# Row maxima over 8 tiles of 112 queries in place of 7 tiles of 128, in a fused cross-attention and expert kernel on one core

## The chip, the core and the metric

The kernel runs on one core of a Trainium2 chip. Times are device microseconds (us). The engines are TensorE (PE, its weight loads PEld), VectorE (DVE), ScalarE (ACT), GpSimd (POOL) and SyncE (SP), which issues most of the DMAs.

## The reference, cut to what matters

```python
q = layernorm(x) @ Wq.T + bq                  # x: 16 batches x 224 queries x 512
k, v = ctx @ Wk.T + bk, ctx @ Wv.T + bv       # ctx: 16 x 750 keys x 384
attn = softmax(einsum('bihd,bjhd->bhij', q, k) * SCALE)   # 16 heads of 32
x = x + (einsum('bhij,bjhd->bihd', attn, v) @ Wo.T + bo)
x = x + top2_of_8_experts(layernorm(x))       # routing, gelu, two matmuls per expert
```

The softmax subtracts the maximum of each row (one query of one head, over 750 keys) before the exponential.

## The kernel before, in words

Attention takes about three quarters of the time; routing and the experts follow and are not touched. Attention is cut into 64 groups: 16 batches by 4 groups of 4 heads. Each engine has its program written out by hand: four functions named `first`, `second`, `third` and `fourth` say what an engine does for a group with index 0, 1, 2 or 3 within its batch, and a loop over g from -2 to 68 calls them in turn. Semaphores are the only tie between engines, and each engine works strictly in the order of its program.

In iteration g the PE works on three groups at once:

- group g: `score(g, s)`, twelve steps of two matmuls each into one of two banks S (125 keys by 224 queries, for one head), which ACT turns into probabilities `pr` (`exps`, L781). Step s waits until ACT has read step s-2. `values(g, p)` multiplies the probabilities by v into O (16 small matmuls, L1558); `denominators(g - 1)` (L1569) waits for sums of the probabilities that POOL adds up (`add_step`, L475 and L478).
- group g+1: `score_for_max(g + 1, u)` (L1519) computes approximate scores with queries on the partitions, only to get the maxima. The 4 heads by 224 queries are 896 rows, cut into 7 tiles u of 128. A tile takes two matmuls of 376 keys each (a pair) into X, which is a single buffer of two banks: DVE's `maximum` (L1061) reduces both to one column of `mx`, and the next pair waits for that (`max_done`). After the last tile `transpose_max` (L1528) turns `mx` into rows in a bank of M; ACT negates them into `mneg` (L771), and a DMA from SP (`put_max`, L390) puts them as one row of 896 numbers under the stacked queries `qst`, so that the score matmuls of the next iteration subtract the maximum by themselves. `score(g + 1, 0)` waits for this DMA.
- group g+2: the projections of q and k, and once a batch v and the output (`project_q`, `project_k`, `project_v`, `project_o`, with their three matmuls a product at L314 to L316).

The order of `score_for_max` among the rest is written out. In all four functions tile 0 comes at or near the start and tile 6 about four fifths through; `transpose_max` stands next to the last scores. What stands between tile 6 and the transpose differs: `values(g, 1)` and scores everywhere, and besides the logits of the router in `first` (L1462), half of the output projection in `second`, transposes of y in `fourth` (L1447). Below, the part from tile 6 to the transpose is called the tail of a function, and the whole of what `score_for_max` adds for one u is a pair.

`q_own` (written by ACT, `own_done`) holds, for each of the 4 heads of a group, the group's queries with the other heads' rows set to zero. It is laid out as head, then query, so that a tile of 128 rows runs over the border between heads in some places.

Of the kernel before, what the change touches and what calls it, by code (L numbers as in the profile page):

```python
# [64 lines left out]
GROUPS = B * NG  # L65
SB, MB = 2, 3
OS = 5
XU = GH * NQ // P
LAST = 5
LN_STEPS, Y_STEPS = 8, 16  # L70
E, DE = 8, 256
# [48 lines left out]
def expert_phase(nc, x1_d, w1, b1, w2, b2, centroids, w_route, ident_d, gates_dram, out):  # L120
    x, ctxT, wqT, bq, wkT, bk, wvT, bv, woT, bo, ident, x1 = SCRATCH["attention"]
    with ExitStack() as es:
# [45 lines left out]
        y_T = sb("y_T", [P, DC, NQ])  # L168
        o_s = sb("o_s", [P, NQ])
        rw = sb("rw", [P, DC, 2 * E])  # L170
        mneg = sb("mneg", [XU, P], F32R)
        zone_end = here[0]

        bq_s, bk_s, bv_s = sb("bq_s", [P, NG]), sb("bk_s", [P, NG]), sb("bv_s", [P, NG])
# [159 lines left out]
        with nc.Block() as block:  # L334
# [350 lines left out]
            def _(act):  # L685
# [79 lines left out]
                def max_out(g):  # L765
                    if not 0 <= g < GROUPS:
                        return
                    wait_full(act, "mT", g)
                    if g:
                        act.wait_ge(m_in, 16 * g)  # L770
                    act.activation(mneg[:, :], bank_of("mT", g)[0:XU, 0:P], ACT.Copy, scale=-1.0).then_inc(freed("mT", g), 1)  # L771

                def exps(g, s):
                    if not 0 <= g < GROUPS:
# [235 lines left out]
            def _(dve):  # L1010
# [44 lines left out]
                def maximum(g, u):  # L1055
                    if not 0 <= g < GROUPS:
                        return
                    if u == 0 and g:
                        wait_full(dve, "mT", g - 1)
                    dve.wait_ge(x_full, XU * g + u + 1)  # L1060
                    dve.tensor_reduce(mx[:, u:u + 1], X[:, :, 0:HALF[0][1]], AX.XY, ALU.max).then_inc(max_done, 1)  # L1061

                def invert(g):
                    if not 0 <= g < GROUPS:
# [92 lines left out]
                def first(g, b):  # L1157
                    maximum(g + 1, 0)
                    q_lo(g + 2)
                    maximum(g + 1, 1)  # L1160
                    maximum(g + 1, 2)
                    k_lo(g + 2, 0)
                    maximum(g + 1, 3)
                    k_lo(g + 2, 1)
                    invert(g - 1)
                    normalise(g - 1)
                    maximum(g + 1, 4)
                    o_lo(g - 1)
                    maximum(g + 1, 5)
                    maximum(g + 1, 6)  # L1170
                    keep_logits(b - 2, 0)
                    keep_logits(b - 2, 1)

                def second(g, b):
                    maximum(g + 1, 0)
                    q_lo(g + 2)
                    maximum(g + 1, 1)
                    maximum(g + 1, 2)
                    k_lo(g + 2, 0)
                    maximum(g + 1, 3)  # L1180
                    k_lo(g + 2, 1)
                    xT_rest(b + 1, 0)
                    xT_rest(b + 1, 1)
                    invert(g - 1)
                    normalise(g - 1)
                    maximum(g + 1, 4)
                    o_lo(g - 1)
                    maximum(g + 1, 5)
                    residual(b - 1, 0)
                    maximum(g + 1, 6)  # L1190
                    residual(b - 1, 1)

                def third(g, b):
                    maximum(g + 1, 0)
                    q_lo(g + 2)
                    maximum(g + 1, 1)
                    maximum(g + 1, 2)
                    k_lo(g + 2, 0)
                    maximum(g + 1, 3)
                    k_lo(g + 2, 1)  # L1200
                    invert(g - 1)
                    normalise(g - 1)
                    maximum(g + 1, 4)
                    o_lo(g - 1)
                    maximum(g + 1, 5)
                    maximum(g + 1, 6)
                    y_stats(b - 1)

                def fourth(g, b):
                    maximum(g + 1, 0)  # L1210
                    q_lo(g + 2)
                    maximum(g + 1, 1)
                    maximum(g + 1, 2)
                    k_lo(g + 2, 0)
                    maximum(g + 1, 3)
                    k_lo(g + 2, 1)
                    invert(g - 1)
                    normalise(g - 1)
                    maximum(g + 1, 4)
                    o_lo(g - 1)  # L1220
                    maximum(g + 1, 5)
                    maximum(g + 1, 6)
                    ln_stats(b + 2)

                for g in range(-2, GROUPS + LAST):
# [193 lines left out]
            def _(pe):  # L1419
# [89 lines left out]
                def score_for_max(g, u):  # L1509
                    if not 0 <= g < GROUPS:  # L1510
                        return
                    own_q = q_own[:, g % 2, :, :].rearrange("p j n -> p (j n)")
                    if u == 0:
                        pe.wait_ge(kh_done, 2 * (g + 1))
                    pe.wait_ge(own_done, GH * g + (P * (u + 1) - 1) // NQ + 1)
                    if g or u:
                        pe.wait_ge(max_done, XU * g + u)
                    for i, (off, w) in enumerate(HALF):
                        last = pe.matmul(X[:, i, 0:w], own_q[:, P * u:P * (u + 1)],  # L1519
                                         kh_s[:, g % 2, off:off + w], start=True, stop=True)  # L1520
                    last.then_inc(x_full, 1)

                def transpose_max(g):
                    if not 0 <= g < GROUPS:
                        return
                    out, full = claim("mT", g)
                    pe.wait_ge(max_done, XU * (g + 1))
                    pe.transpose(out[0:XU, 0:P], mx[:, :], id_s[:, :]).then_inc(full, 1)  # L1528

                def score(g, s):  # L1530
                    if not 0 <= g < GROUPS:
# [75 lines left out]

                def first(g, b):
                    score_for_max(g + 1, 0)
                    project_q(g + 2)  # L1610
                    project_k(g + 2, 0)
                    score_for_max(g + 1, 1)
                    values(g - 1, 2)
                    score(g, 0)
                    score(g, 1)
                    score_for_max(g + 1, 2)
                    project_k(g + 2, 1)
                    score_for_max(g + 1, 3)
                    score(g, 2)
                    denominators(g - 1)  # L1620
                    project_v(b, 4, 0)
                    score_for_max(g + 1, 4)
                    score(g, 3)
                    score(g, 4)
                    project_v(b, 4, 1)
                    project_v(b, 5, 0)
                    score(g, 5)
                    project_v(b, 5, 1)
                    score_for_max(g + 1, 5)
                    score(g, 6)  # L1630
                    score(g, 7)
                    values(g, 0)
                    score(g, 8)
                    score_for_max(g + 1, 6)
                    values(g, 1)
                    score(g, 9)
                    logits(b - 2, 0)
                    logits(b - 2, 1)
                    score(g, 10)
                    score(g, 11)  # L1640
                    transpose_max(g + 1)

                def second(g, b):
# [26 lines left out]
                    score_for_max(g + 1, 6)  # L1670
                    project_o(b - 1, 1, 0)
                    score(g, 9)
                    project_o(b - 1, 1, 1)
                    score(g, 10)
                    score(g, 11)
# [2 lines left out]
                def third(g, b):  # L1678
                    project_q(g + 2)
                    score_for_max(g + 1, 0)  # L1680
                    project_k(g + 2, 0)
                    score_for_max(g + 1, 1)
                    score(g, 0)
                    values(g - 1, 2)
                    score(g, 1)
                    score_for_max(g + 1, 2)
                    project_k(g + 2, 1)
                    score(g, 2)
                    score_for_max(g + 1, 3)
                    project_v(b + 1, 0, 0)  # L1690
                    project_v(b + 1, 0, 1)
                    score(g, 3)
                    denominators(g - 1)
                    score_for_max(g + 1, 4)
                    project_v(b + 1, 1, 0)
                    score(g, 4)
                    score(g, 5)
                    project_v(b + 1, 1, 1)
                    score_for_max(g + 1, 5)
                    values(g, 0)  # L1700
                    score(g, 6)
                    score_for_max(g + 1, 6)
                    score(g, 7)
                    score(g, 8)
                    score(g, 9)
                    values(g, 1)
                    score(g, 10)
                    transpose_max(g + 1)
                    score(g, 11)

                def fourth(g, b):
# [27 lines left out]
                    score(g, 9)  # L1739
                    transpose_y(b - 1, 0)  # L1740
                    transpose_y(b - 1, 1)
                    score(g, 10)
                    transpose_max(g + 1)
                    score(g, 11)
# [125 lines left out]
```

## Time and profile before

| | |
|---|---|
| median of 3 runs | 1679.36 us (1679.16 to 1681.23) |
| the profiled execution | 1679.16 us, of which the span from first to last instruction is 1677.3 us |
| granted TensorE clock, mean over the span | 0.962 of full speed |
| PE busy | 1532.5 us, 91% |
| POOL / DVE / ACT busy | 65% / 58% / 56% |
| first and last pair of the row maxima | from 34.0 us to 1280.4 us |

The trace's times count from the span's start. A busy PE is not a PE at its peak, since matmuls overlap: the distance from one matmul's start to the next one's is what it costs in a row of them.

### The profile page before, as it was taken

To read this page: it belongs to the slowest core of one execution; us is meant where nothing else is said; L and a number is where in the kernel's file an instruction comes from. 1 tells how busy PE (TensorE), PEld (TensorE's weight loads), DVE (VectorE), ACT (ScalarE), POOL (GpSimd) and SP (SyncE) were. 2 spreads that over 40 slices of the span, in tenths; PEclk is the share of its full clock that TensorE was granted. 3 is DMA by queue.
4 is the path that set the end of the run, shared out by engine and by line. 5 is a ranking of instruction groups with operands and counts; after the bars stand their busy time and mean duration, and the time that the engine had idled before them with its cause. 6 is when DMAs were issued, how large, how long until landed. Compare 5 with 4: busy or idle time off the path is not lost.

```text
span 1677.3 us, 32844 instructions
## 1 busy us (share of the span) xinstructions
PE 1532.5 (91%) x11581; PEld 1256.8 (75%) x11581; DVE 973.8 (58%) x1464; ACT 935.6 (56%) x2048; POOL 1091.4 (65%) x947
## 2 busy tenths in 40 slices
PE   4899999999999999999999999999996439998997
PEld 4778787877877777778787877877774328887886
DVE  6555666566565656655666566565654574444665
ACT  4556665665666566666666666666554403553332
POOL 3377767767767777676767767777765514766553
PEclk9999999999999999999999999999997658998999
DMA  7564767676667676665767676657666416887663
GB/s 194 98 111 76 135 101 130 101 133 106 122 103 132 102 130 102 118 122 95 136 101 130 102 131 109 122 100 133 91 102 153 164 25 145 148 143 149 217 202 119
DMA packets 111372, 206.90 MB, mean 123 GB/s; under 512 B 19391, under 2 KB 48671, under 8 KB 111088
## 3 DMA queue, kind: packets, MB, share of 16 engines
q1 hardware_dynamic: 95456, 160.18, 52.2%
q0 software_dynamic: 15760, 44.63, 11.5%
q8 instruction: 100, 1.64, 0.4%
q14 instruction: 56, 0.46, 0.1%
HBM read 75.60 MB, written 35.00 MB: 66 GB/s over the span
## 4 chain that ended last, share of the span: by engine, by line
PE 63%; POOL 17%; issue 8%; ACT 4%; DVE 3%; DMA 3%; SPq 2%; POOLq 0%; DVEq 0%; ACTq 0%
POOL psum_p L478 11%; PE M L314 8%; PE S L1542 8%; PE M L315 8%; PE M L316 8%; PE X L1519 7%; PE O L1558 7%; POOL ctx_l L462 3%; ACT pr L781 2%; PE M L1569 2%; PE X L1782 2%; PE X L1781 2%; PE X L1783 2%; PE M L1802 1%; PE M L1800 1%
## 5 line engine op out<-in xcount | busy, mean ns | idle before, releaser
L478 POOL TENSOR_TENSOR psum_p<-psum_p,pr 125x896 f32<-125x896 f32 x256 | 542.3, 2118 | 174.1 <-ACT pr L781 150.8
L1061 DVE TENSOR_REDUCE mx<-X 128x1 f32<-128x752 f32 x448 | 421.4, 941 | 365.4 <-PE X L1519 363.3
L781 ACT ACTIVATE pr<-S 125x448 f32<-125x448 f32 x768 | 394.7, 544 | 215.7 <-PE S L1542 202.5
L1542 PEld LDWEIGHTS S<-qst,kst 128*125 128x125 f32 x1536 | 235.0, 189 | 123.7 <-ACT pr L781 60.0
L1542 PE MATMUL S<-qst,kst 128*125 128x224 f32 x1536 | 286.8, 291 | 39.1 <-ACT pr L781 26.5
L1519 PE MATMUL X<-kh_s,q_own 128*128 128x376 f32 x896 | 242.9, 352 | 5.5 <-DVE mx L1061 5.4
L1558 PE MATMUL O<-pr,v 125*32 125x224 f32 x3072 | 187.0, 362 | 1.9 <-ACT pr L781 1.9
L475 POOL TENSOR_TENSOR psum_p<-pr 125x896 f32<-125x896 f32 x64 | 135.1, 2112 | 82.1 <-ACT pr L781 81.9
L1519 PEld LDWEIGHTS X<-kh_s,q_own 128*128 128x128 f32 x896 | 146.5, 191 | 43.9 <-issue 34.8
L462 POOL TENSOR_TENSOR ctx_l<-ctx_r,ctx_h 128x750 fp32r<-128x750 f32 x48 | 85.3, 1807 | 75.8 <-ACT ctx_h L696 75.8
L314 PE MATMUL M<-ctx_h,wk_h 128*128 128x376 f32 (+1 forms) x384 | 128.9, 336 | 0.2 <-POOL ctx_l L462 0.2
L315 PE MATMUL M<-ctx_l,wk_h 128*128 128x376 f32 (+1 forms) x384 | 128.7, 335 | 0.0
L316 PE MATMUL M<-ctx_h,wk_l 128*128 128x376 f32 (+1 forms) x384 | 128.0, 333 | 0.0
L1068 DVE RECIPROCAL M<-M 128x224 f32<-128x224 f32 x64 | 99.8, 1560 | 47.8 <-PE M L1569 47.8
L1558 PEld LDWEIGHTS O<-pr,v 125*32 125x32 f32 x3072 | 80.8, 110 | 58.6 <-issue 21.2
L314 PE MATMUL M<-wv_h,ctx_h 128*125 128x512 f32 x288 | 116.9, 406 | 0.0
L315 PE MATMUL M<-wv_l,ctx_h 128*125 128x512 f32 x288 | 113.8, 395 | 0.0
L316 PE MATMUL M<-wv_h,ctx_l 128*125 128x512 f32 x288 | 113.6, 394 | 0.0
L738 ACT ACTIVATE q_own<-qh_s,own 128x224 fp32r<-128x224 f32 x256 | 102.6, 471 | 2.1
L1388 DVE TENSOR_TENSOR y_raw<-M,b_all 128x512 f32<-128x512 f32 x70 | 48.4, 692 | 83.6 <-PE M L1802 83.6
L632 POOL DMA_INDIRECT xg<-rows_d,table_x x40 | 41.9, 1048 | 76.4 <-ACT y_out L991 42.3
L1051 DVE SCALAR_TENSOR_TENSOR kl_s<-M,bk_s,kh_s 128x376 fp32r<-128x376 f32 (+1 forms) x128 | 77.2, 603 | 15.0 <-ACT kh_s L749 14.0
(217 smaller groups left out, 3161.5 us busy)
## 6 DMA issues: line engine op xcount, KB each, us to landing
kst<-kh_s SPq DMA_DIRECT2D x128, 375.0 KB, 7.4
kst<-kl_s SPq DMA_DIRECT2D x64, 375.0 KB, 10.4
ctx_r<-ctxT SPq DMA_DIRECT2D x48, 375.0 KB, 12.3
qst<-qh_s SPq DMA_DIRECT2D x128, 112.0 KB, 2.8
rows_d<-x_res SPq DMA_DIRECT2D x32, 448.0 KB, 11.4
w_l<-w SPq DMA_DIRECT2D x16, 512.0 KB, 10.0
x_ln<-x SPq DMA_DIRECT2D x16, 448.0 KB, 11.1
x_res<-x SPq DMA_DIRECT2D x16, 448.0 KB, 3.6
```

Source lines behind the costliest of these rows:

```text
L314: pe.matmul(out, lhs[0], rhs[0], start=first, stop=False)
L315: pe.matmul(out, lhs[0], rhs[1], start=False, stop=False)
L316: return pe.matmul(out, lhs[1], rhs[0], start=False, stop=last)
L462: pool.tensor_tensor(out=ctx_l[:, c, :], in0=ctx_r[:, c, :], in1=ctx_h[:, c, :], op=ALU.subtract).then_inc(ctx_lo, 1)
L475: pool.tensor_tensor(out=total, in0=tiles[0], in1=tiles[1], op=ALU.add).then_inc(sum_step, 1)
L478: pool.tensor_tensor(out=total, in0=total, in1=tiles[half], op=ALU.add).then_inc(sum_step, 1)
L738: act.activation(q_own[:, g % 2, j, :], qh_s[:, g % 2, :], ACT.Copy, scale=own[:, j:j + 1]).then_inc(own_done, 1)
L781: act.activation(pr[0:KP, (3 * g + p) % 2, j, :, :], S[0:KP, n % SB, 0:2 * NQ].rearrange("p (i n) -> p i n", i=2), ACT.Exp).then_inc(exp_d ...
L1061: dve.tensor_reduce(mx[:, u:u + 1], X[:, :, 0:HALF[0][1]], AX.XY, ALU.max).then_inc(max_done, 1)
L1519: last = pe.matmul(X[:, i, 0:w], own_q[:, P * u:P * (u + 1)], kh_s[:, g % 2, off:off + w], start=True, stop=True)
L1542: last = pe.matmul(S[0:KP, n % SB, NQ * h:NQ * (h + 1)], kst[:, i, j, o:o + KP], qst[:, i, j, :], start=True, stop=True)
L1558: last = pe.matmul(O[HD * j:HD * (j + 1), 0:NQ], v[0:KP, 2 * p + i, HD * j:HD * (j + 1)], pr[0:KP, (3 * g + p) % 2, j, i, :], start=(p == ...
```

## The change

The 896 rows are cut into 8 tiles of 112: tile u is head u // 2, half u % 2. The number of tiles `XU` goes from 7 to 8, matmuls, reduce, transpose and `mneg` work on 112 columns or partitions where they had 128, and each function of PE and DVE gets one more call, for u = 7. A tile lies within one head, so `own_done` is waited for only where a head begins.

```diff
-XU = GH * NQ // P
+XU = 8
-        mneg = sb("mneg", [XU, P], F32R)
+        mneg = sb("mneg", [XU, QP], F32R)
...
-                    dve.tensor_reduce(mx[:, u:u + 1], X[:, :, 0:HALF[0][1]], AX.XY, ALU.max).then_inc(max_done, 1)
+                    dve.tensor_reduce(mx[0:QP, u:u + 1], X[0:QP, :, 0:HALF[0][1]], AX.XY, ALU.max).then_inc(max_done, 1)
...
-                    own_q = q_own[:, g % 2, :, :].rearrange("p j n -> p (j n)")
+                    j, qt = u // QT, u % QT
                     if u == 0:
                         pe.wait_ge(kh_done, 2 * (g + 1))
-                    pe.wait_ge(own_done, GH * g + (P * (u + 1) - 1) // NQ + 1)
+                    if qt == 0:
+                        pe.wait_ge(own_done, GH * g + j + 1)
                     if g or u:
                         pe.wait_ge(max_done, XU * g + u)
                     for i, (off, w) in enumerate(HALF):
-                        last = pe.matmul(X[:, i, 0:w], own_q[:, P * u:P * (u + 1)],
+                        last = pe.matmul(X[0:QP, i, 0:w], q_own[:, g % 2, j, QP * qt:QP * (qt + 1)],
                                          kh_s[:, g % 2, off:off + w], start=True, stop=True)
...
-                    pe.transpose(out[0:XU, 0:P], mx[:, :], id_s[:, :]).then_inc(full, 1)
+                    pe.transpose(out[0:XU, 0:QP], mx[0:QP, :], id_s[0:QP, 0:QP]).then_inc(full, 1)
...
# DVE, at the end of each of the four functions, ahead of keep_logits, residual 1, y_stats, ln_stats:
                     maximum(g + 1, 6)
+                    maximum(g + 1, 7)
...
# PE, first, second (after score 9), third (after score 9), fourth (after transpose_y):
                     score(g, 9)
+                    score_for_max(g + 1, 7)
```

The PE's instructions at the end of `third`, from score 9 to the transpose, before:

```order
L1542 MATMUL S<-qst,kst 125x224 [waits exp_done]
L1542 MATMUL S<-qst,kst 125x224
L1558 MATMUL O<-pr,v_70 32x224 [waits exp_done]
L1558 MATMUL O<-pr,v_70 32x224 x7
L1542 MATMUL S<-qst,kst 125x224 [waits exp_done]
L1542 MATMUL S<-qst,kst 125x224
L1528 MATMUL M<-id_s,mx 7x128 [waits max_done,misc_free2]
```

and now:

```order
L1547 MATMUL S<-qst,kst 125x224 [waits exp_done]
L1547 MATMUL S<-qst,kst 125x224
L1524 MATMUL X<-kh_s,q_own 112x376 [waits max_done]
L1524 MATMUL X<-kh_s,q_own 112x376
L1563 MATMUL O<-pr,v_70 32x224 [waits exp_done]
L1563 MATMUL O<-pr,v_70 32x224 x7
L1547 MATMUL S<-qst,kst 125x224 [waits exp_done]
L1547 MATMUL S<-qst,kst 125x224
L1533 MATMUL M<-id_s,mx 8x112 [waits max_done,misc_free2]
```

A pair has come in ahead of `values(g, 1)`; between it and the transpose stand those matmuls and one score. At the end of `fourth` the PE has, before:

```order
L1447 MATMUL M<-id_s,x_res 128x112 [waits yn_done,misc_free1]
L1447 MATMUL M<-id_s,x_res 128x112 x3
L1542 MATMUL S<-qst,kst 125x224 [waits exp_done]
L1542 MATMUL S<-qst,kst 125x224
L1528 MATMUL M<-id_s,mx 7x128 [waits max_done,misc_free2]
```

and now, with the new pair between the transposes of y and score 10:

```order
L1451 MATMUL M<-id_s,x_res 128x112 [waits yn_done,misc_free1]
L1451 MATMUL M<-id_s,x_res 128x112 x3
L1524 MATMUL X<-kh_s,q_own 112x376 [waits max_done]
L1524 MATMUL X<-kh_s,q_own 112x376
L1547 MATMUL S<-qst,kst 125x224 [waits exp_done]
L1547 MATMUL S<-qst,kst 125x224
L1533 MATMUL M<-id_s,mx 8x112 [waits max_done,misc_free2]
```

## Rows read from the trace of the kernel before

**Rows 1.** The page: the chain that ended last, share of the span by engine.
```profile
PE 63%; POOL 17%; issue 8%; ACT 4%; DVE 3%; DMA 3%; SPq 2%; POOLq 0%; DVEq 0%; ACTq 0%
```
**Rows 2.** The page's groups: line, operation, count, busy and mean, idle before by releaser.
```profile
L1061 DVE TENSOR_REDUCE mx<-X 128x1 f32<-128x752 f32 x448 | 421.4, 941 | 365.4 <-PE X L1519 363.3
...
L1519 PE MATMUL X<-kh_s,q_own 128*128 128x376 f32 x896 | 242.9, 352 | 5.5 <-DVE mx L1061 5.4
```
**Rows 3.** Waits within attention (33 to 1285 us): total, times, longest.
```profile
PEld S L1542 <- issue: 40.9, 111, 1.1
PEld X L1519 <- issue: 34.8, 82, 1.6
...
PE S L1542 <- ACT pr L781: 23.9, 39, 2.3
```
**Rows 4.** The chain in order of time, `fourth`: start, us, what (x2 is one pair).
```profile
815.63 0.55 PE X L1519 x2
...
817.72 0.35 PE X L1519 x2
```
**Rows 5.** Timeline, end of `first`, PE and DVE: start, us, instruction, count [idle before].
```profile
849.04 0.94 DVE L1061 TENSOR_REDUCE mx<-X 128x1 f32<-128x752 f32 x1 [1.14 <-PE X L1519]
...
849.83 0.48 PE L1542 MATMUL S<-qst,kst 128*125 128x224 f32 x2
850.14 1.65 PE L1462 MATMUL M<-rw,y_T 128*112 128x16 f32 x16
...
852.15 0.27 PE L1528 MATMUL M<-id_s,mx 128*7 128x128 f32 x1
```
**Rows 6.** Timeline, PE, end of `second`.
```profile
870.59 0.38 PE L1542 MATMUL S<-qst,kst 128*125 128x224 f32 x2
...
872.62 0.27 PE L1528 MATMUL M<-id_s,mx 128*7 128x128 f32 x1
```
**Rows 7.** Timeline, end of `third`, PE and DVE.
```profile
809.96 1.48 PE L1542 MATMUL S<-qst,kst 128*125 128x224 f32 x6
...
810.15 0.94 DVE L1061 TENSOR_REDUCE mx<-X 128x1 f32<-128x752 f32 x1 [0.77 <-PE X L1519]
...
811.37 0.96 PE L1558 MATMUL O<-pr,v 125*32 125x224 f32 x16
...
812.58 0.27 PE L1528 MATMUL M<-id_s,mx 128*7 128x128 f32 x1
```
**Rows 8.** Timeline, PE, end of `fourth`.
```profile
830.11 0.93 PE L1447 MATMUL M<-id_s,x_res 112*128 112x112 f32 x8
832.22 0.48 PE L1542 MATMUL S<-qst,kst 128*125 128x224 f32 x2 [1.18 <-ACT pr L781]
832.53 0.27 PE L1528 MATMUL M<-id_s,mx 128*7 128x128 f32 x1
```
**Rows 9.** Timeline, middle of `third`, POOL and PE at the denominators.
```profile
795.17 8.88 POOL L478 TENSOR_TENSOR psum_p<-psum_p,pr 125x896 f32<-125x896 f32 x4
...
803.70 0.37 PE L1542 MATMUL S<-qst,kst 128*125 128x224 f32 x2
804.20 0.59 PE L1569 MATMUL M<-psum_p,ones 125*32 125x224 f32 x8
```
**Rows 10.** Timeline, PE and DVE, the maxima of group 0 (no scores yet).
```profile
46.28 0.59 PE L1519 MATMUL X<-kh_s,q_own 128*128 128x376 f32 x2 [1.12 <-DVE mx L1061]
46.91 0.94 DVE L1061 TENSOR_REDUCE mx<-X 128x1 f32<-128x752 f32 x1 [0.77 <-PE X L1519]
47.99 0.37 PE L1528 MATMUL M<-id_s,mx 128*7 128x128 f32 x1 [1.12 <-DVE mx L1061]
```
**Rows 11.** Busy time by engine in a stretch; after POOL the granted clock.
```profile
48.00:51.40 3.40, 3.40 (x15) 3.36 (x16) 2.17 (x6) 0.27 (x1) 1.53 (x5) 0.50 0.10 35
```
**Rows 12.** Groups of weight loads by shape (400 to 1200 us), busy and mean ns.
```profile
L1519 PEld LDWEIGHTS X<-kh_s,q_own 128*128 128x128 f32 x570 | 92.4, 190 | 23.5 <-issue 18.6
...
L315 PEld LDWEIGHTS M<-wo_l,oT_h 128*112 128x112 f32 x80 | 14.0, 175 | 2.3
```

More of the change, by code:

```diff
@@ L770, in max_out @@
                         act.wait_ge(m_in, 16 * g)
-                    act.activation(mneg[:, :], bank_of("mT", g)[0:XU, 0:P], ACT.Copy, scale=-1.0).then_inc(freed("mT", g), 1)
+                    act.activation(mneg[:, :], bank_of("mT", g)[0:XU, 0:QP], ACT.Copy, scale=-1.0).then_inc(freed("mT", g), 1)
                 def exps(g, s):
@@ L1190, in second @@
                     maximum(g + 1, 6)
+                    maximum(g + 1, 7)
                     residual(b - 1, 1)
@@ L1206, in third @@
                     maximum(g + 1, 6)
+                    maximum(g + 1, 7)
                     y_stats(b - 1)
@@ L1222, in fourth @@
                     maximum(g + 1, 6)
+                    maximum(g + 1, 7)
                     ln_stats(b + 2)
@@ L1672, in second @@
                     score(g, 9)
+                    score_for_max(g + 1, 7)
                     project_o(b - 1, 1, 1)
@@ L1705, in third @@
                     score(g, 9)
+                    score_for_max(g + 1, 7)
                     values(g, 1)
@@ L1741, in fourth @@
                     transpose_y(b - 1, 1)
+                    score_for_max(g + 1, 7)
                     score(g, 10)
```

## Prediction

> **What bounds the kernel now.** I read the chain that ended last first, then the idle times beside the groups, then the waits within attention, and last the timeline of the four tails. The chain lies on the PE for 63% of the span [rows 1]. DVE, which takes the maxima, is no bound: its 448 reduces of 0.941 us each were preceded by 363 us of waiting for PE's pairs, while PE waited for a reduce for only 5.4 us in all [rows 2]. The PE within attention loses little: 23.9 us to ACT's exponentials in 39 waits [rows 3]. The reader is to see that the PE is a full queue there, and that a matmul added to it costs its own place unless it falls just ahead of one of the few waits. So I ask of each of the four tails whether the new pair stands ahead of a wait, and whether the transpose behind it must now wait for the eighth reduce.
>
> **What a pair costs.** In the chain a pair takes 0.35 us in a row of matmuls and 0.55 us behind the small matmuls of O [rows 4]. The moving side stays at 376 columns, so 112 stationary columns in place of 128 give nothing back, and seven old pairs cost what they did.
>
> **What the transpose waits for.** The rows of group 0 show the bare chain: pair at 46.28, reduce at 46.91, transpose at 47.99, with nothing between [rows 10]. From the pair's start to the earliest transpose it is 1.71 us: 0.63 to the reduce, 0.94 of reduce, 0.14 to the PE. With the new pair last, this is a new condition in each tail. X is one buffer, so the new pair must also wait until reduce 6 has ended, plus those 0.14 us.
>
> **Tail of first, 16 times.** Score 9 starts at 849.83, the logits at 850.14, so the pair would start at about 850.04 to 850.14. Reduce 6 starts at 849.04, and 0.94 and 0.14 later, at 850.12, X is free [rows 5]: a wait of at most 0.08. The transpose would be at 852.15 plus the pair, far behind 850.12 + 1.71 = 851.83. No PE wait follows, so the pair costs 0.35 to 0.55; I take 0.45, since it has the wait for X and a change of operands beside the 0.35: 7.2 us.
>
> **Tail of second, 16 times.** Score 9 starts at 870.59, the pair some 0.2 later at 870.8, the transpose was at 872.62 [rows 6]; 870.8 + 1.71 = 872.51 holds nothing up. Projections stand around it, so 0.40: 6.4 us. But part comes back at once. In the middle of third the PE stands before the denominators: its score pair starts at 803.70, the denominators at 804.20, just behind the end of four POOL additions, 795.17 + 8.88 = 804.05 [rows 9]. Two score matmuls with a change of operands behind them take 850.14 - 849.83 = 0.31 elsewhere [rows 5], so about 0.2 of the 0.50 here is waiting for POOL. POOL's row of work there starts before the new pair of second, so it doesn't move, and the PE arrives 0.40 later at a place where it waited 0.2: minus 0.2 each, minus 3.2 us.
>
> **Tail of third, 15 times.** The pair comes between score 9 and O. The six score matmuls from 809.96 include waits for ACT, O starts at 811.37 [rows 7]; a good 0.1 to 0.2 of the time ahead of O is the change to its small matmuls and the pair can stand in it. Reduce 6 ends at 811.09, X is free at 811.23, which is about where the pair would start. Its earliest transpose is 811.23 + 1.71 = 812.94 against 812.58 before: 0.36. By PE's queue alone it would be 0.25 to 0.35. I take 0.33: 5.0 us. Here the reduce and not the PE's queue sets the end, with little between them. There are 16 thirds; the last has the maxima of group 63, which are followed by weight loads of the experts in SP's queue, and I leave it out (0.33 at most).
>
> **Tail of fourth, 15 times.** Score 10 stands still for 1.18 us until ACT has read bank S [rows 8]. The transposes of y start at 830.11 and take 0.93 with their own latency, so a pair at about 830.85 is over by 831.2, inside the wait that ends at 832.22: PE pays nothing. The transpose of the maxima can be at 830.85 + 1.71 = 832.56, against 832.53. I take 0.05: 0.8 us. If that cover were gone, 0.4 each, 6 us.
>
> **Start, once.** For group 0 (a fourth) there are no scores; pairs 5 and 6 already alternate with their reduces, 46.28 to 47.99 [rows 10]. One more turn is 1.7 us. Right behind it the PE runs at the lower of its two levels of granted clock, 1.2 GHz (0.50 of full from 48.0 to 51.4), after a stretch in which it mostly waited [rows 11]. A longer wait could lengthen that by some of a like stretch: 0 to 1.7 us, of which I take nothing into the sum and keep the end.
>
> **Other parts.** 64 more reduces (60 us of DVE) go into DVE's waiting time; behind them in its queue stand keep_logits, the second residual, y_stats and ln_stats, which feed POOL and ACT later in the next iteration; they move by about a microsecond and nothing waits for them that soon. The row of maxima goes to SP as 8 pieces in place of 7 of the same total. The dropped waits for q_own cost nothing now, since q_own is written an iteration ahead; zero for them, below nothing in the last rival.
>
> **The sum.** 7.2 + 6.4 - 3.2 + 5.0 + 0.8 + 1.7 = 17.9 us; a cycle of four groups gets longer by 0.45 + 0.40 - 0.20 + 0.33 + 0.05 = 1.03. Against the profiled execution's own 1679.16 us (2 us of it outside the span; the median of the runs, 1679.36, is the same within 0.02%) I forecast 1679.2 + 17.9, rounded to 1697. Low end: 0.35 in first and 0.35 in second, of which POOL's wait swallows 0.3, 0.2 in third, nothing in fourth: 0.60 x 16 + 1.7 = 11.3, 1690.5. High end: 0.55, 0.45 without anything given back, 0.45, 0.1 and the clock: 1.55 x 16 + 3.4 = 28.2, 1707.4.
>
> **Rivals.**
> - *Every pair is paid in full.* POOL's work shifts along with the PE, and fourth's gap closes because ACT's row shifts too. For it: ACT runs its last four exponentials right behind y. Against it: the gap is a wait for ACT that starts before the new pair. 64 x 0.45 + 1.7 = 30.5, so 1709.7. Chance 7%.
> - *Weights set the pace.* If 112 columns lost a faster way of loading, each of the 1024 matmuls for maxima would stretch from a place of 0.17 us (half a pair) to the 0.19 us of its load: 1024 x 0.02 = 20 us on top, 1717. Against it: loads of 112 columns take 175 ns and of 128 columns 190 ns [rows 12]; they get shorter, and both are pipelined. Chance 2%. The Trainium skill (TensorE: Matmul & The Clock Gate, Weight-path perf modes) says that fast weight load is on only with 128 weights and a type that isn't FP32, a rule that speaks against this change if these fp32r operands had it; the trace's two load times don't look like a mode that 112 columns lack.
> - *No change to be measured.* If loads and not moving columns set PE's pace in these pairs, then 8 x 112 = 7 x 128 columns are loaded and only the start's 1.7 us are left: 1681. Against it: pairs of 0.35 us against 2 x 190 ns of load. Chance 3%. The Trainium skill (TensorE: Matmul & The Clock Gate, LDWEIGHTS) has the load time go with the columns, as rows 12 bear out in direction: 15 ns less for 16 columns.
> - *The reduce sets every tail.* DVE gets to reduce 7 late, because in second the residual, in the others bn_stats of the iteration before stand in its queue, and X frees late: each tail then shows the full 1.71 us less what lies between. With 1 us exposed in each: 64 + 18 = 82, 1761. It decides once the reduce starts 0.5 us behind its pair or more. Against it: DVE waits before nearly each reduce. Chance 2%.
> - *Faster.* The PE's weight loads ahead of pairs idled for "issue" 82 times, 34.8 us in all [rows 3]. If waiting for q_own beside max_done made this, and it went wholly with the change, the time would be 1697.0 - 34.8 = 1662; from more than half of it the kernel is faster. Against it: the loads of the score matmuls, which never wait for q_own, idle in the same way, 111 times [rows 3], and the change drops only every second such wait. Chance 2%.
>
> **Chances and range.** The forecast's own case has 84%, the rivals 7, 2, 3, 2 and 2%. The ends of the first case are 1690.5 and 1707.4; trimmed to 8 in 10, with the rivals outside, 1690 to 1705. A difference of 0.2% (3.4 us) is about what a measurement of this kernel can tell from none. Faster 2%, within it 3%, slower 95%.
>
> **What would show it.** In the profile after: 1024 matmuls for X with the same 0.35 us in the chain and reduces still of 0.94 us; the tails of first, second and third longer by 0.45, 0.40 and 0.33 us; the wait before the denominators in third gone; score 10 in fourth at the same distance from the pair of u = 6, with its wait shorter; at the start one more 1.7 us turn. The forecast is wrong if fourth is longer by 0.3 us or more, if the transpose waits for a reduce in first or second, or if pairs differ from 0.35 us.

## The result and the profile after

The change is slower: 1694.07 us median (1690.98 to 1695.97, 4 runs) against 1680.3 (1679.16 to 1682.3, 4 runs), a ratio of 1.0079 with a 95% interval of 1.0059 to 1.0099. The profiled execution took 1696.22 us, 1694.4 of it the span, 17.1 us more than the one before. The forecast was 1697.0.

The page of the changed kernel, its busy times and two of its groups (columns as in [rows 2]):

```profile
PE 1554.1 (92%) x11709; PEld 1272.1 (75%) x11709; DVE 1053.0 (62%) x1528; ACT 936.6 (55%) x2048; POOL 1088.6 (64%) x947
...
L1061 DVE TENSOR_REDUCE mx<-X 112x1 f32<-112x752 f32 x512 | 480.5, 938 | 356.0 <-PE X L1524 353.9
...
L1524 PE MATMUL X<-kh_s,q_own 128*112 128x376 f32 x1024 | 272.3, 347 | 8.2 <-DVE mx L1061 8.0
```

A reduce takes 938 ns where it took 941, and DVE took the 64 more out of its waits [rows 2].

The best clock inside the trace is the transpose of the maxima, one a group. The distance from one to the next, as a mean over the 13 or 14 transposes of each kind from group 6 to 60, is what I call the period of a function below (spread about 0.01 to 0.08 us):

| us | first | second | third | fourth | cycle | transpose of group 5 at |
|---|---|---|---|---|---|---|
| before | 19.62 | 20.43 | 18.70 | 19.96 | 78.71 | 143.8 |
| after | 19.92 | 20.69 | 18.68 | 19.94 | 79.23 | 151.1 |

A cycle is longer by 0.52, or 8.4 us over 16 cycles. By the transpose of group 5, 7.3 us are lost already; after group 5, and up to group 61, another 7.3; nearly all of the rest, 2.3 us, lies behind the last transpose, in the part that was not touched.

The timeline of the changed kernel's PE in the tails of third, fourth and first, in this order; they answer to [rows 7], [rows 8] and [rows 5]:

```profile
822.79 0.50 PE L1524 MATMUL X<-kh_s,q_own 128*112 128x376 f32 x2
823.23 0.96 PE L1563 MATMUL O<-pr,v 125*32 125x224 f32 x16
824.12 0.48 PE L1547 MATMUL S<-qst,kst 128*125 128x224 f32 x2
824.43 0.26 PE L1533 MATMUL M<-id_s,mx 112*8 112x112 f32 x1
...
841.94 0.93 PE L1451 MATMUL M<-id_s,x_res 112*128 112x112 f32 x8
842.64 0.57 PE L1524 MATMUL X<-kh_s,q_own 128*112 128x376 f32 x2
844.05 0.48 PE L1547 MATMUL S<-qst,kst 128*125 128x224 f32 x2 [0.84 <-ACT pr L781]
844.37 0.26 PE L1533 MATMUL M<-id_s,mx 112*8 112x112 f32 x1
...
861.94 0.50 PE L1524 MATMUL X<-kh_s,q_own 128*112 128x376 f32 x2
862.28 1.65 PE L1466 MATMUL M<-rw,y_T 128*112 128x16 f32 x16
...
864.30 0.26 PE L1533 MATMUL M<-id_s,mx 112*8 112x112 f32 x1
```

In fourth the pair has gone into the wait for ACT, which is now 0.84 us where it was 1.18. In first it takes 862.28 - 861.94 = 0.34. In third the transpose comes 1.64 us behind the pair, with matmuls all the way. It stands 0.31 us behind the start of the scores ahead of it, as it did before, so it doesn't wait for the reduce; but it misses that wait by little, since the eighth reduce ended only 0.16 us earlier (mean of 14). And the middle of third, which answers to [rows 9]:

```profile
815.50 0.37 PE L1547 MATMUL S<-qst,kst 128*125 128x224 f32 x2
815.80 0.59 PE L1574 MATMUL M<-psum_p,ones 125*32 125x224 f32 x8
```

From the scores to the denominators it is 0.30 us where it was 0.50: the wait for POOL is gone.

### The profile page after: what moved, and what is told of

Read it like the earlier page. It is cut to its first block, busy times and chain, and to the rows that moved or that the text cites. A ratio compares the mean times of both kernels' runs of the same rounds, so it can differ in the third digit from the quotient of the medians.

```text
span 1694.4 us, 32972 instructions
## 1 busy us (share of the span) xinstructions
PE 1554.1 (92%) x11709; PEld 1272.1 (75%) x11709; DVE 1053.0 (62%) x1528; ACT 936.6 (55%) x2048; POOL 1088.6 (64%) x947
## 3 DMA queue, kind: packets, MB, share of 16 engines
q8 instruction: 100, 1.64, 0.5%
## 4 chain that ended last, share of the span: by engine, by line
PE 80%; ACT 4%; DVE 4%; DMA 4%; POOL 3%; issue 3%; SPq 2%; DVEq 0%; POOLq 0%; ACTq 0%
PE M L314 11%; PE S L1547 11%; PE M L315 11%; PE M L316 11%; PE X L1524 10%; PE O L1563 10%; ACT pr L781 2%; PE M L1574 2%; PE X L1791 1%; PE X L1790 1%; PE X L1792 1%; DMA xg<-rows_d,table_t 1%; POOL psum_p L478 1%; PE M L1811 1%; PE M L1809 1%
## 5 line engine op out<-in xcount | busy, mean ns | idle before, releaser
L1061 DVE TENSOR_REDUCE mx<-X 112x1 f32<-112x752 f32 x512 | 480.5, 938 | 356.0 <-PE X L1524 353.9
L1524 PE MATMUL X<-kh_s,q_own 128*112 128x376 f32 x1024 | 272.3, 347 | 8.2 <-DVE mx L1061 8.0
L1524 PEld LDWEIGHTS X<-kh_s,q_own 128*112 128x112 f32 x1024 | 154.2, 177 | 47.8 <-issue 26.5
L632 POOL DMA_INDIRECT xg<-rows_d,table_x x40 | 41.9, 1048 | 77.4 <-ACT y_out L991 41.8
## 6 DMA issues: line engine op xcount, KB each, us to landing
rows_d<-x_res SPq DMA_DIRECT2D x32, 448.0 KB, 10.8
```

What stands on the lines that cost most here:

```text
L1061: dve.tensor_reduce(mx[0:QP, u:u + 1], X[0:QP, :, 0:HALF[0][1]], AX.XY, ALU.max).then_inc(max_done, 1)
L1524: last = pe.matmul(X[0:QP, i, 0:w], q_own[:, g % 2, j, QP * qt:QP * (qt + 1)], kh_s[:, g % 2, off:off + w], start=True, stop=True)
```

## The experiments

All ratios are to the kernel before, run on the same chip; three chips took part, on which the kernel before had medians of 1684.05, 1684.21 and 1683.79.

### What in the change costs: pair, width, waits

`dup128` is the kernel before with an eighth pair of 128 columns, cut here to its main lines.

```diff
-                    pe.wait_ge(own_done, GH * g + (P * (u + 1) - 1) // NQ + 1)
+                    pe.wait_ge(own_done, GH * g + (P * (min(u, XU - 1) + 1) - 1) // NQ + 1)
-                        last = pe.matmul(X[:, i, 0:w], own_q[:, P * u:P * (u + 1)],
+                        last = pe.matmul(X[:, i, 0:w], own_q[:, P * v:P * (v + 1)],     # v = min(u, 6)
```

> The kernel before (7 tiles of 128, all its waits for q_own) with an eighth pair of 128 columns in the same four places; it computes tile 6 again and its maximum goes to a column nobody reads. The theory that only the added pair counts: a cycle of four groups, 78.7 us before and 79.2 after, is 79.2 again within 0.05, and the median is within 3 us of the change's 1694. The rival that narrower tiles and dropped waits gave something back: a cycle of 79.3 to 79.5 and 2 to 5 us more than the change.

Measured: ratio 1.0106 (1.0086 to 1.0125), 1703.02 us; periods 20.03, 20.79, 18.83, 19.97, a cycle of 79.62. The rival holds, and the cycle is even above its 79.3 to 79.5: the pair alone lengthens a cycle by 0.92, more than the whole change does.

`waits_back` is the change with all its waits.

```diff
-                    if qt == 0:
-                        pe.wait_ge(own_done, GH * g + j + 1)
+                    pe.wait_ge(own_done, GH * g + j + 1)
```

> The change, with the wait for q_own back at all eight tiles. If the dropped waits explain why second grew by 0.26 us and not by 0.35, second grows by 0.05 to 0.1 here, and 256 waits cost 1 to 3 us in all. If they cost nothing, every period is the change's within 0.02 us.

Measured: ratio 1.0088 (1.0069 to 1.0107); periods 19.98, 20.76, 18.76, 19.95, a cycle of 79.46. So of the 0.92, narrow tiles give back 0.17 and the dropped waits 0.22 (16 waits a cycle), 2.7 and 3.6 us over 16 cycles. These two come from the periods alone, since the intervals of the three ratios overlap; that such waits cost device time, `once_before` shows below. The gain isn't spread evenly. The tail of first in `dup128`, on the PE:

```profile
866.42 0.48 PE L1549 MATMUL S<-qst,kst 128*125 128x224 f32 x2
866.74 0.58 PE L1526 MATMUL X<-kh_s,q_own 128*128 128x376 f32 x2
867.16 1.65 PE L1468 MATMUL M<-rw,y_T 128*112 128x16 f32 x16
```

With both waits the pair takes 0.42 from its start to the next instruction, where with one it takes 0.34; the records of `waits_back` have 0.40 at this place. Only four of the 16 pairs that lost the wait show more than 0.02 between `waits_back` and the change: this one (0.055), tile 1 in second and tile 5 in third (0.06 each, with the projections ahead of them), and tile 7 in third (0.02). What they share is in the traces of DVE: in the change these four pairs start 0.06 to 0.18 us after the reduce that frees X for them has ended, and the other twelve 0.33 us after it or later. So they are the pairs whose other wait, for `max_done`, is met only just. It isn't what stands ahead of them: tile 5 in third has six projections of 512 columns ahead, which at 0.23 us each are as long as any matmul in attention.

The price shows where the reduce alone holds the pair up. The new pair of group 0 starts 0.145 us after its reduce has ended with both waits (`waits_back`), and 0.054 with one (the change); tile 5 in third does so 0.15 and 0.06 us after. The wait for `q_own` is long met there, and still adds 0.09 us behind the reduce.

`once_before` is the kernel before, 7 tiles, with that wait once a group:

```diff
                     if u == 0:
                         pe.wait_ge(kh_done, 2 * (g + 1))
-                    pe.wait_ge(own_done, GH * g + (P * (u + 1) - 1) // NQ + 1)
+                        pe.wait_ge(own_done, GH * (g + 1))
```

> The kernel before (7 tiles), with the wait for q_own taken once a group, at tile 0, for all four heads. If a wait beside the other costs the PE something where it stands behind O, a cycle of 78.71 us gets shorter by 0.1 to 0.2 and the kernel by 1.5 to 3 us; if not, both are the same within 0.02 us and 0.1%.

Measured: ratio 0.9981 (0.9971 to 0.9991); periods 19.62, 20.35, 18.59, 19.96, a cycle of 78.52, 0.19 shorter. The groups of weight loads for X, first of `once_before`:

```profile
L1519 PEld LDWEIGHTS X<-kh_s,q_own 128*128 128x128 f32 x896 | 145.5, 190 | 41.9 <-DVE mx L1061 23.6 <-issue 10.8
```

and of the kernel before:

```profile
L1519 PEld LDWEIGHTS X<-kh_s,q_own 128*128 128x128 f32 x896 | 146.5, 191 | 43.9 <-issue 34.8 <-ACT q_own L738 1.2
```

The idle time that was put down to "issue" falls from 34.8 to 10.8 us, but most of it only gets another name: 41.9 us of idle time in all stand against 43.9. A label of a wait is not a gain. The places are of the same kind as before: tile 1 in second and tiles 5 and 6 in third, which start 0.15 to 0.16 us after their reduce in the kernel before, get 0.05 to 0.07 shorter, with what stands just ahead of them, and no other pair gains 0.02.

A second run on another chip, `once_before2`:

> The kernel before with the wait for q_own once a group, a second time, on this chip: a cycle of 78.52 within 0.02, and a ratio to the kernel before of 0.997 to 0.999, so that it is the fastest of all. The rival: the first ratio, 0.9981, came from the clock in the first 100 us, and it is 1.000 here.

Measured: ratio 0.9972 (0.9958 to 0.9985), a cycle of 78.55. It is the fastest kernel of the study, twice clear of the kernel before, by 0.2 to 0.3%.

`once_after` is the same edit in the change:

```diff
-                    if qt == 0:
-                        pe.wait_ge(own_done, GH * g + j + 1)
+                        pe.wait_ge(own_done, GH * (g + 1))      # inside if u == 0
```

> The change (8 tiles of 112), with the wait for q_own once a group at tile 0 for all heads. The waits at tiles 2, 4 and 6 are the ones left to drop. If a second wait costs the PE only where few or short matmuls are queued ahead of it, third gets 0.04 to 0.08 shorter (tile 6 comes right behind one score) and the others stay: a cycle of 79.15 to 79.2. If each wait costs the same, the 4 waits dropped by the change having given 0.225 a cycle over 16 places, these 12 give 0.17: 79.06.

Measured: ratio 1.0056 (1.0044 to 1.0069); periods 19.92, 20.69, 18.64, 19.91, a cycle of 79.15. The place decides, not the count: the pair of tile 6 in third goes from 0.395 to 0.346 us, O and that pair in fourth from 0.967 + 0.497 to 0.904 + 0.527, and no other place moves by 0.01. Of the twelve pairs these two are the only ones that started less than 0.3 us after their reduce (as means 0.16 and 0.15). That fourth gained 0.03 was not foreseen as a place, though the total was.

### Where the pair is paid, and where it comes back

In three kernels the new pair and its reduce are cut to 16 keys a half in one function, so that the semaphores stay as they are. The edit of the matmuls, with the group of the maxima that second works on (3 for third, 0 for fourth, there without group 0):

```diff
                     for i, (off, w) in enumerate(HALF):
+                        w = 16 if u == 7 and g % NG == 2 else w
```

> The change, with the eighth pair and its reduce cut to 16 keys a half in second alone (16 keys a half stand for the last half head's maximum there). My theory of the return: second gets 0.3 shorter, and third, 18.68 now, gets 0.2 to 0.25 longer, since the PE waits for POOL ahead of the denominators again; the cycle falls by 0.05 to 0.1 only. The rival, that each pair is paid on its own and third's 18.68 has another cause: second 0.3 shorter, third unchanged, the cycle 0.3 less.

The PE in the middle of third, in `light_second`:

```profile
813.29 0.37 PE L1549 MATMUL S<-qst,kst 128*125 128x224 f32 x2
813.73 0.58 PE L1576 MATMUL M<-psum_p,ones 125*32 125x224 f32 x8
```

Measured: 1694.79 us (one run); periods 19.93, 20.55, 18.79, 19.97, a cycle of 79.23, the same as with the full pair. Second saves 0.14 us (a pair of 16 keys still takes 0.13, and the projections behind it 0.07 more). Third loses 0.10 of it at once, by a wait of 0.12 before the denominators (as a mean 0.42 here, 0.30 in the change), and fourth the other 0.03, at O and the pair of tile 6. My theory of the return holds; only the sizes were too large, since a light pair isn't free.

> The change, with the eighth pair and its reduce cut to 16 keys a half in third alone. If the pair's place on the PE sets the cost, third falls from 18.68 to about 18.4 (0.3 less); if the wait of the transpose for the reduce set it, the same or up to 0.05 more comes back; if third's pair is hidden and the wait for POOL is not what it replaced, third stays at 18.68.

Measured: 1692.89 us (one run); third 18.45, fourth 19.89, a cycle of 78.94. The tail of third in `light_third`:

```profile
818.97 0.48 PE L1549 MATMUL S<-qst,kst 128*125 128x224 f32 x2
819.29 0.27 PE L1526 MATMUL X<-kh_s,q_own 128*112 128x16 f32 x2
819.49 0.96 PE L1565 MATMUL O<-pr,v 125*32 125x224 f32 x16
```

The pair takes 0.20 here and 0.44 in the change; the difference is the difference of the period, 0.24. So the pair's place on the PE is the cost, and neither the transpose nor the reduce. Fourth gets 0.05 shorter as well, which I didn't expect: O and the pair behind it take 0.894 + 0.526 in place of 0.967 + 0.497.

What couples the two functions shows on DVE and POOL. In fourth DVE writes `oT_l` (L1082) just ahead of the reduce of tile 5. The two engines in the kernel before, then in the changed one:

```profile
824.88 0.44 DVE L1082 SCALAR_TENSOR_TENSOR oT_l<-o_s,bv_s,oT_h 128x224 fp32r<-128x224 f32 x1
825.33 2.10 POOL L475 TENSOR_TENSOR psum_p<-pr 125x896 f32<-125x896 f32 x1
```

```profile
836.71 2.30 DVE L1082 SCALAR_TENSOR_TENSOR oT_l<-o_s,bv_s,oT_h 128x224 fp32r<-128x224 f32 x1
836.65 2.11 POOL L475 TENSOR_TENSOR psum_p<-pr 125x896 f32<-125x896 f32 x1
```

Where DVE's instruction starts 0.45 us ahead of POOL's addition, it takes 0.44 us; where it starts just behind, it lasts until 0.25 us after the addition's end. So it is in every fourth from group 6 on, in all 13 traces: 0.44 us in `light_third`, `light_all` and the kernels with 7 tiles, 2.2 to 2.4 us in the others. The reduce of tile 5 then starts late, ends 1.69 us behind the start of its pair in place of 1.49, and the pair of tile 6 starts 0.15 us after it. So the new pair in third shifts DVE against POOL, and fourth pays for it on the PE. That the one engine stretches the other's instruction is read from this timing; no run takes POOL's addition away.

> The change, with the eighth pair and its reduce cut to 16 keys a half in fourth alone (except for group 0). My theory: the pair lies in the PE's wait for ACT and costs nothing, so fourth stays at 19.94 within 0.03 us. The rival, paid in full: 0.3 shorter.

Measured: 1696.19 us (one run); fourth 19.96, a cycle of 79.25. The pair in fourth is free.

`light_all` has the light pair in every group.

> The change, with the eighth pair and its reduce cut to 16 keys a half for every group. If only the pair's matmuls cost time and the dropped waits and narrower tiles give back about 0.2 to 0.4 a cycle, the cycle is 78.4 to 78.7 (78.71 before, 79.23 with the change) and the time that of the kernel before within 4 us, start included. If the eighth reduce, its semaphore round trip or the eighth row of maxima cost something of their own, the cycle stays at 78.9 or above.

Measured: ratio 1.0007 (0.9997 to 1.0017), 1685.92 us; a cycle of 78.76. It is within 0.2% of the kernel before, so the columns of the pair and its reduce are the loss, less what narrow tiles and dropped waits give back. The cycle is just above the upper end that I gave and below 78.9: the semaphores and the eighth row cost nothing that shows. The reduce is cut here too, so this kernel doesn't acquit it; that it isn't the cost comes from `light_third`, and from first and second, where the transpose comes 0.87 and 0.68 us after the eighth reduce has ended.

### The first 100 us

`light_start` has the light pair for the maxima of groups 0 to 5 alone (`u == 7 and g < 6`).

> The change, with the eighth pair and its reduce cut to 16 keys for the maxima of groups 0 to 5 only (so 16 keys in each half stand for the last half head's maximum there). In the trace 7.3 us of the 17 are lost by the transpose of group 5. My theory: few matmuls stand around the pairs there, the PE waits for the reduce, and the lower clock is granted for longer; with the light pair 4 to 6 us of the 7.3 come back, and steady periods stay. The rival, that this part is drift between executions: no more than the pairs' own 1.5 us comes back.

Measured: ratio 1.0060 (1.0042 to 1.0078) against the change's 1.0079; the transpose of group 5 at 147.5 us, 3.6 of the 7.3 back, just under the 4 to 6 that I expected. The cycle is 79.25. The PE of the changed kernel while group 2's maxima are made, in second of the first batch, which has no output projection yet:

```profile
90.83 0.60 PE L1524 MATMUL X<-kh_s,q_own 128*112 128x376 f32 x2 [0.82 <-DVE mx L1061]
91.27 0.59 PE L1547 MATMUL S<-qst,kst 128*125 128x224 f32 x4
92.55 0.26 PE L1533 MATMUL M<-id_s,mx 112*8 112x112 f32 x1 [0.70 <-DVE mx L1061]
```

Here the pair and the transpose do wait for the reduces, 1.5 us together; the transpose of group 1, at 71.07, waits 0.35. The granted clock tells the other part. The stretch from 33 to 150 us of the kernel before, then of the changed one (after POOL comes the granted clock):

```profile
33.00:150.00 117.00, 108.61 (x799) 87.91 (x798) 64.10 (x88) 67.45 (x155) 62.84 (x46) 0.97 0.62 102
```

```profile
33.00:150.00 117.00, 107.32 (x760) 86.44 (x758) 65.76 (x89) 63.45 (x145) 56.04 (x42) 0.94 0.60 98
```

0.03 of the full clock over 117 us, at half of full speed, is 7 us more at 1.2 GHz, worth 3.5. That worth is an estimate. `light_start` and `light_all` are one program up to group 5, and they stand there at 147.5 and 145.3 us, with 13.6 and 6.8 us of the lower clock by then in their traces: 2.2 us for 6.8, and not 3.4.

Counted from the first pair, which leaves out what varies ahead of it, the transpose of group 5 comes after 109.8 us in the kernel before, 110.6 in `light_all`, 112.8 in `light_start` and 116.7 in the change. So of the 6.9 us between the first and the last, 4.0 are the full columns of pairs and reduces (`light_start` and the change have the same 13.6 us of the lower clock), 2.2 the longer stretch at the lower clock, and 0.8 what stays with light pairs. The clock differs between two executions of one program, as those two show; but all five traces of kernels in which each eighth pair is full have 13.6 us of it by group 5, and all three of kernels with 7 tiles 3.4 or 6.8. So the change has a share in it; how large a share is open.

The change once more, `after_again`:

> The change itself, once more, beside the other two of this set and the kernel before on one chip. Expected: a cycle of 79.23 again within 0.02 and a ratio of 1.007 to 1.010. If the 7.3 us lost by the transpose of group 5 were drift, that part would be another one here by several us; if it belongs to the change, 6 to 8.

Measured: ratio 1.0080 (1.0067 to 1.0093), a cycle of 79.26, the transpose of group 5 at 152.0 us, 8.3 us behind the profiled execution before, a little over the 6 to 8 that I gave; from the first pair on it is 116.7 us again. It repeats. The stretch from the last transpose to the end, untouched, took 393.9 us before, and 396.3 and 397.1 in the two runs of the change, but 396.2 and 397.4 in the two of `once_before` and 390.5 in `once_after`: it varies by itself, so its 2.3 us in the profiled pair are not a cost of the change that is shown.

## Why the prediction was right

The direction held, slower by a time inside the range (1690 to 1705), and so did the main mechanism: a pair in first, second or third takes its place in the PE's queue, one in fourth is hidden. That the total came as near as 17.1 us against 17.9 was luck, since two large errors cancelled (below). By its steps:

- **What bounds it.** Held. `light_all`, which cuts the columns of the eighth pairs and of their reduces, is back at the kernel before (1.0007), and the transposes of a full cycle wait for no reduce.
- **Tail of first.** Forecast 0.45, measured 0.30. With both waits and 128 columns, as I had priced it, it is 0.41 (`dup128`).
- **Tail of second, and the return.** Forecast 0.40 less 0.20. Second grew by 0.26 (0.36 in `dup128`), and the whole wait for POOL, 0.25 as a mean, came back. `light_second` shows the return by itself.
- **Tail of third.** Forecast 0.33 with the reduce setting the end. The size held (0.34 for pair and scores together), the reason fell: the reduce doesn't hold the transpose up, and `light_third` gets back just the 0.24 by which the pair's place on the PE shrinks. The chain of 1.71 us, taken from group 0, was too long here: the reduce starts 0.54 us behind its pair and not 0.63.
- **Tail of fourth.** Forecast 0.05; measured -0.02, and `light_fourth` gives 0.02 the other way. The pair is hidden. What I had not seen is that the pair in third costs fourth 0.05 by way of POOL and DVE, for which the working has no term.
- **The steps that failed** are two that I set to zero, "the dropped waits for q_own cost nothing now" and "112 stationary columns in place of 128 give nothing back". They gave 0.22 and 0.17 us a cycle, 6.3 us in all. I had argued from the data's being there; but the second wait adds up to 0.09 us where the reduce frees X only just in time, though `q_own` is long there.
- **Start.** The term was sized at 1.7 us; by the transpose of group 5 it was 7.3, some 4 us of it from the chain that I had seen for group 0 only, and 2.2 with the lower clock, for which I had taken nothing. Groups 1 to 4 lack other matmuls too, since the output projection, the logits and the transposes of y begin later: the transposes of groups 1 to 4 come 0.14 to 0.16 us after their last reduce.

The sum came out near because the two errors oppose: 16 cycles gave 8.4 us where 16.2 was forecast, and start and end 8.7 where 1.7 was, 2.3 of it in the untouched end, which varies by itself. The cycle of `dup128`, 0.92 against my 1.03, is what the working itself was worth.

Of the rivals, "every pair is paid in full" is out by `light_second` and `light_fourth`; "the reduce sets every tail" holds up to group 5 only; weights setting the pace is out both ways: loads of 112 columns got shorter (177 ns for 190) and the matmuls' places didn't grow. The "faster" rival had a true half: the second wait costs something, 3.6 us here and not 34.8.

The Trainium skill's rule on fast loads (TensorE: Matmul & The Clock Gate, Weight-path perf modes) would have made loads of 112 columns slower than of 128, had it applied to these fp32r operands; the trace has 177 ns against 190 and shows no sign of it.

## What to carry to other kernels

Where one engine's queue is full, price an added instruction by the place it takes there, but look at what lies just behind: ahead of a wait for another engine it is free (fourth), and behind it a later wait gives it back (second into third). A second semaphore on an instruction is not free just because it is always met: here it added up to 0.09 us where the other was met only just. Take such a wait once, on an instruction that isn't released by another engine at the last moment. Look at the engines off the path too: a shift of a few tenths of a microsecond put an instruction of DVE behind one of POOL, at five times its length. And look at the first rounds of a pipeline apart: there the fillers that hide a chain are missing.

## What was not expected of the hardware

- A second wait, long met, adds 0.09 us to a pair that the reduce releases: it starts 0.145 us after the reduce's end with two waits and 0.054 with one (group 0, `waits_back` and the change). Where the reduce ended 0.33 us ahead or more, it cost at most 0.01.
- A DVE instruction of 0.44 us takes 2.30 when it starts 0.06 us behind the start of a POOL addition of 2.11 us (`oT_l` in fourth, before and after).
- A pair with 112 stationary columns takes up to 0.02 us less than one with 128 in most places (0.397 against 0.411 in first's tail, `waits_back` and `dup128`). Over a cycle of 32 pairs that is 0.17 us.
- A pair of 16 columns a half takes 0.13 us, and the projections behind it in second (`light_second`) or the logits in first (`light_all`) take 0.07 us longer: together more than half of the 0.34 that a pair of 376 takes.
- The same program up to 145 us was granted the lower of the two clocks for 6.8 us in one execution and 13.6 in another, and took 2.2 us longer with it (`light_all` and `light_start`).
